# Attention values on half the TensorE columns, with unsplit F32 rows and a ring of probability tiles

## What is computed

```python
q_big = rope(einsum('bshk,hkq->bshq', (hidden_q @ Wq.T), w_kc_q))       # 192 per head
kv_r = rope(kv_c)                                                       # 1444 x 64
scores = einsum('bhsr,bhlr->bhsl', q_big @ W_qr, kv_r @ W_kr)
attn = softmax(scores)
ctx_c = einsum('bhsl,bld->bhsd', attn, kv_r)
out = reshape(einsum('bhsd,hkd->bhsk', ctx_c, w_kc_kv)) @ Wo.T
```

## Time and profile before

| | us |
|---|---|
| median of 3 runs | 2302.54 |
| the profiled execution, its own time | 2283.25 |
| its span | 2281.4 |
| PE busy | 1857.9 (81%) |
| PEld busy | 1632.6 (72%) |
| DVE busy | 1492.1 (65%) |
| ACT busy | 1220.5 (53%) |
| POOL busy | 1117.1 (49%) |

### The profile page before, as it was taken

The page is one execution under the profiler, slowest core; times in us unless marked ns, Lnnn a source line. Parts: engine busy times, 40 slices in busy tenths (PEclk is TensorE's granted clock), DMA queues, the critical chain, the costliest instruction groups (busy, mean ns, idle before and its releaser), DMA issues. The chain is left out here.

```text
span 2281.4 us, 38538 instructions
## 1 busy us (share of the span) xinstructions
PE 1857.9 (81%) x10550; PEld 1632.6 (72%) x10550; DVE 1492.1 (65%) x2799; ACT 1220.5 (53%) x2996; POOL 1117.1 (49%) x961
## 2 busy tenths in 40 slices
PE   4999958999999999999999973499993689837870
PEld 3677736888888888888888963499993466626870
DVE  4677777777777777767776433377774466656763
ACT  2111115777777767767777851366661266515650
POOL 0455528888788888878888852300004100014005
PEclk9999967999999999999999985699996599958985
DMA  5522251111111111111110002455542100026654
GB/s 159 197 58 57 55 176 55 63 63 63 45 54 63 64 31 63 63 64 63 63 54 11 16 8 78 140 197 196 204 165 58 34 1 0 0 77 196 198 164 113
DMA packets 115748, 195.76 MB, mean 86 GB/s; under 512 B 48213, under 2 KB 94265, under 8 KB 110161
## 3 DMA queue, kind: packets, MB, share of 16 engines
q1 hardware_dynamic: 107409, 180.88, 24.6%
q0 software_dynamic: 8192, 13.15, 2.0%
HBM read 147.01 MB, written 46.63 MB: 85 GB/s over the span
## 5 line engine op out<-in xcount | busy, mean ns | idle before, releaser
L501 POOL TENSOR_TENSOR EL<-E,EH 128x400 fp32r<-128x400 f32 x688 | 833.4, 1239 | 158.5 <-ACT EH L733 154.0
L599 DVE TENSOR_REDUCE PM<-bank 128x1 f32<-128x482 f32 (+1 forms) x624 | 397.2, 650 | 185.9 <-PE bank L578 182.9
L742 ACT ACTIVATE E<-bank 128x400 f32<-128x400 f32 x768 | 386.4, 503 | 212.8 <-PE bank L793 153.2
L733 ACT ACTIVATE EH<-E 128x400 fp32r<-128x400 f32 x768 | 407.0, 532 | 0.0
L175 PE MATMUL bank<-EH,KVH 128*128 128x400 f32 x768 | 283.1, 369 | 19.8 <-POOL EL L501 18.5
L578 PE MATMUL bank<-KH,QS 128*128 128x482 f32 (+1 forms) x624 | 250.9, 414 | 53.9 <-DVE KVL L549 27.6
L1248 POOL DMA_INDIRECT m_back<-rows_out,m_slots x64 | 64.8, 1013 | 450.8 <-DMA rows_out<-m_ys 421.2
L792 PE MATMUL bank<-QS,KH 128*128 128x400 f32 x768 | 272.1, 354 | 14.9 <-issue 9.1
L793 PE MATMUL bank<-QB,KB 66*128 66x400 f32 x768 | 269.1, 350 | 0.0
L175 PE MATMUL bank<-EH,KVL 128*128 128x400 f32 x768 | 265.7, 346 | 0.0
L175 PE MATMUL bank<-EL,KVH 128*128 128x400 f32 x768 | 265.5, 346 | 0.0
(11 more groups left out here) (244 smaller groups left out, 3983.3 us busy)
## 6 DMA issues: line engine op xcount, KB each, us to landing
m_stage_u<-in_m_up SPq DMA_DIRECT2D x20, 1392.0 KB
raw<-in_ctx_T SPq DMA_DIRECT2D x16, 1444.0 KB, 6.1
m_xg<-rows_in SPq DMA_DIRECT2D x55, 256.0 KB, 4.1
rows_out<-m_ys SPq DMA_DIRECT2D x55, 256.0 KB, 3.7
m_stage_d<-in_m_down SPq DMA_DIRECT2D x20, 696.0 KB
queries<-q_out SPq DMA_DIRECT2D x64, 200.0 KB, 2.4
QS<-queries SPq DMA_DIRECT2D x16, 800.0 KB, 6.1
rows_in<-zeros SPq DMA_DIRECT2D x5, 1792.0 KB
```

Of the source, the lines that this page charges most:

```text
L501: ops.tensor_tensor(EL[:, n % PB, :], E[:, n % EB, :], as_f32(EH[:, n % PB, :]), ALU.subtract).then_inc(sem, 1)
L599: nc.vector.tensor_reduce(PM[:, f:f + 1], psum[F0 + f % f_banks(b)][:, 0:KW[f % KC]], AX.X, ALU.max).then_inc(red_done, 1)
L733: nc.scalar.activation(EH[:, n % PB, :], E[:, n % EB, :], ACT.Copy).then_inc(hi_done, 1)
L742: nc.scalar.activation(E[:, n % EB, :], psum[S0 + n % SB][:, 0:CH], ACT.Exp).then_inc(exp_done, 1)
```

## The change

1. PSUM is one tensor `banks`, so that one instruction can read two banks.
2. Queries: `M2` keeps 64 columns a head. `narrow` takes two heads at a time, head `2j` to PSUM rows 0 to 63 and head `2j+1` to rows 64 to 127. ScalarE and VectorE then take a pair in one instruction of 128 rows, and four DMAs of 64 rows send it.
3. Attention: a step is a tile of 128 keys by 800 columns, even heads in one bank and odd heads in the next (24 steps). One exponential of 128x800 writes both into the ring `R`, where the four tiles of a group and a running sum lie innermost, so neighbouring columns stand 20 bytes apart. No `EH`, `EL`.
4. `values`: two F32 matmuls of 400 columns with 64 stationary columns, even heads to PSUM rows 0 to 63, odd heads to rows 64 to 127 of one bank `CTX`, from `KV` in F32.
5. Row sums: VectorE sums the even heads, four parts of 100 columns for each group of four tiles (`sum_even`); GpSimd adds the odd heads tile by tile (`sum_odd`); TensorE adds over the partitions with a matrix of ones (`sums`).
6. Maxima: two pieces of 482 columns in two banks, one `tensor_reduce` over both (`reduce_pair`, 20 instead of 39). With two banks in all, a pair waits for the reduction of the pair before.
7. Ten rotation parts go to GpSimd, two stay on VectorE. `KB` and `QB` have 128 rows, with a row that masks the padded keys, and the setup clears them.

The core of the diff:

```diff
@@ latent_queries
-                def narrow(c, h):
-                    pe.wait_ge(rot_done, c * H + (BUFS + h + 1))
-                    pe.wait_ge(lo_done, c * H + (h + 1))
+                def narrow(c, j):
+                    pe.wait_ge(rot_done, c * H + (BUFS + 2 * j + 2))
+                    pe.wait_ge(lo_done, c * HP + (j + 1))
                     for half in range(2):
-                        last = nc.tensor.matmul(psum[4 + h % 2][:, 0:CH], M2[:, half, h, :], rot[:, h % TURNS, half, :],
-                                                start=half == 0, stop=half == 1)
+                        for o in range(2):
+                            h = 2 * j + o
+                            last = nc.tensor.matmul(psum[4 + j % 2][o * DC:(o + 1) * DC, 0:CH], M2[:, half, h, :],
+                                                    rot[:, h % TURNS, half, :], start=half == 0, stop=half == 1)
                     last.then_inc(qq_ready, 1)
...
@@ latent_attention
+        def tiles_of(n):
+
+            return R[:, n // GT % 2, :, :, 1 + n % GT]
...
+            nc.vector.tensor_reduce(PM[:, 2 * i:2 * i + n], banks[:, k:k + n, 0:KW], AX.X, ALU.max).then_inc(red_done, 1)
...
+        def sum_even(v, b, g, part):
+
+            cols = slice(part * PC, (part + 1) * PC)
+            p, q = divmod(g, KT // GT)
+            if part == 0:
+                v.wait_ge(exp_done, b_val(b) * NS + ((g + 1) * GT + SB))
+            v.wait_ge(even_sum, b_val(b) * NG * PARTS + (PARTS * (g + 1) + part + 1))
+            src = R[:, g % 2, 0, cols, (1 if q == 0 else 0):]
...
+            nc.vector.tensor_reduce(out, src, AX.X, ALU.add).then_inc(even_sum, 1)
...
+            nc.gpsimd.tensor_tensor(out, first, tile_of(n, 1), ALU.add).then_inc(odd_sum, 1)
...
+            for o in range(2):
+                last = nc.tensor.matmul(psum[MISC][o * DC:(o + 1) * DC, 0:CH], ones[:], ES[:, p, o, :], start=True, stop=True)
+            last.then_inc(sum_done, 1)
...
+        def context_out(act, b, p):
+            act.wait_ge(av_done, b_val(b) * NS + (EB + KT * (p + 1)))
+            act.wait_ge(ct_ready, b_val(b) + 1)
+            nc.scalar.activation(CU[:, p, :], psum[CTX][:, 0:CH], ACT.Copy).then_inc(cu_done, 1)
...
-                    split_products(nc, psum[A0 + g % 2][:, 0:CH],
-                                   [(KVH[b_mod(b)][:, cols], KVL[b_mod(b)][:, cols], EH[:, n % PB, :], EL[:, n % PB, :])],
-                                   first=t == 0, last=t == KT - 1).then_inc(av_done, 1)
+                    for o in range(2):
+                        last = nc.tensor.matmul(psum[CTX][o * DC:(o + 1) * DC, 0:CH], KV[b_mod(b)][:, t, :], tile_of(n, o),
+                                                start=t == 0, stop=t == KT - 1)
+                    last.then_inc(av_done, 1)
...
+                v.wait_ge(rows_set, BUFS)
                 for r in range(BUFS):
+                    v.memset(as_f32(QB[r][0:1, :]), 1.0)
+                    v.memset(as_f32(KB[r][0:3, :]), 1.0).then_inc(rows_set, 1)
+                v.wait_ge(rows_set, 2 * BUFS)
+                for r in range(BUFS):
+                    v.memset(as_f32(KB[r][0:1, 0:SK]), 0.0)
+                    v.memset(as_f32(KB[r][0:1, SK:]), PAD).then_inc(pads, 1)
```

More of the change, by code:

```diff
@@ L52, in __init__ @@
         self.nc, self.ctx = nc, ctx
-        self.psum = [ctx.enter_context(nc.psum_tensor(f"bank{i}", [P, PSUM_COLS], F32)) for i in range(8)]
+        self.banks = ctx.enter_context(nc.psum_tensor("banks", [P, 8, PSUM_COLS], F32))
+        self.psum = [self.banks[:, i, :] for i in range(8)]
         self.stats = fixed(ctx, nc, "stats", [S, B, 6])
@@ L425, in latent_attention @@
-        KVL = [fixed(ctx, nc, f"KVL{r}", [P, KT * KS + P - KS], F32R) for r in range(BUFS)]
+        KB = [fixed(ctx, nc, f"KB{r}", [P, SKP], F32R) for r in range(BUFS)]
+        KV = [fixed(ctx, nc, f"KV{r}", [P, KT, DC]) for r in range(BUFS)]
         raw = fixed(ctx, nc, "raw", [P, 2, SK])
@@ L578, in max_piece @@
-            nc.tensor.matmul(psum[F0 + f % banks][:, 0:KW[j]], QS[r][:, t * P:(t + 1) * P],
-                             KH[r][:, sum(KW[:j]):sum(KW[:j + 1])], start=True, stop=True).then_inc(f_ready, 1)
+                pe.wait_ge(red_done, b_val(b) * NP)
+            for f in pieces(i):
+                t, j = divmod(f, KC)
+                last = nc.tensor.matmul(psum[f_bank(b, i) + f % 2][:, 0:KW], QS[r][:, t * P:(t + 1) * P],
+                                        KH[r][:, KAT[j]:KAT[j] + KW], start=True, stop=True)
@@ L581, in turn_max @@
+            last.then_inc(f_ready, 1)
         def turn_max(pe, b):
@@ new lines, in sum_odd @@
+        def sum_odd(pool, b, n):
+            p, t = divmod(n, KT)
+            if t == 0:
+                return
+            pool.wait_ge(exp_done, b_val(b) * NS + (n + 1 + SB))
+            done = b_val(b) * 2 * ADDS + (p * ADDS + t - 1)
+            if t > 1 or p or b is not FIRST:
+                pool.wait_ge(odd_sum, done)
+            if t == KT - 1 and b is not FIRST:
+                pool.wait_ge(sum_done, b_val(b) * 2 + (p - 1))
+            first = tile_of(n - 1, 1) if t == 1 else EA[:]
+            out = ES[:, p, 1, :] if t == KT - 1 else EA[:]
+            nc.gpsimd.tensor_tensor(out, first, tile_of(n, 1), ALU.add).then_inc(odd_sum, 1)
@@ new lines, in sums, with sums_out @@
+        def sums(pe, b, p):
+            pe.wait_ge(even_sum, b_val(b) * NG * PARTS + (2 * PARTS + PARTS * (NG // 2) * (p + 1)))
+            pe.wait_ge(odd_sum, b_val(b) * 2 * ADDS + ADDS * (p + 1))
+            if p == 0 and b is not FIRST:
+                pe.wait_ge(su_done, b_val(b) * 2)
+            for o in range(2):
+                last = nc.tensor.matmul(psum[MISC][o * DC:(o + 1) * DC, 0:CH], ones[:], ES[:, p, o, :], start=True, stop=True)
+            last.then_inc(sum_done, 1)
+        def sums_out(act, b, p):
+            act.wait_ge(sum_done, b_val(b) * 2 + (p + 1))
+            if b is not FIRST:
+                act.wait_ge(sr_in, b_val(b) * 32)
+            nc.scalar.activation(SU[:, p, :], psum[MISC][0:DC + 1, 0:CH], ACT.Copy).then_inc(su_done, 1)
@@ L668, in steps @@
             body(Batch(0, B - 1), False, False)
+        LAST = Batch(0, B - 1)
         with nc.Block() as block:
@@ L756, in step @@
-                    high(b, NS - 1)
+                            act.wait_ge(odd_sum, odd_sums_to(before(b), NS + n - EB))
+                        k = S0 + 2 * (n % SB)
+                        nc.scalar.activation(tiles_of(n), banks[:, k:k + 2, 0:CH], ACT.Exp).then_inc(exp_done, 1)
+                        if n in HI_AT and has_keys:
+                            keys_high(act, b + 2, HI_AT.index(n))
+                        if n == 2 * SUM_AT + 1 and b is not FIRST:
+                            sums_out(act, before(b), 1)
@@ L784, in step @@
[L784 to L794 removed]
+                        pe.wait_ge(cu_done, b_val(b) * 2 + (p + 1))
@@ L805, in step @@
-                        if n == TURN_AT and has_next:
+                        if has_next and 2 * m < NP:
+                            max_pair(pe, b + 1, 2 * m)
+                        if m == 0:
+                            if b is not FIRST:
+                                for n in range(NS - 2, NS):
+                                    values(before(b), n)
+                            pe.wait_ge(m_in, b_val(b) * 32 + 32)
+                        for n in (2 * m, 2 * m + 1):
+                            scores(b, n)
@@ L808, in step @@
                             turn_max(pe, b + 1)
-                steps(pe, step)
-                for n in range(NS - BEHIND, NS):
-                    values(Batch(0, B - 1), n)
-                project(pe, Batch(0, B - 1))
+                        for n in (2 * m - 2, 2 * m - 1):
+                            if n >= 0:
+                                values(b, n)
+                        if m == SUM_AT and b is not FIRST:
+                            sums(pe, before(b), 1)
+                        if m == SUM0_AT:
+                            sums(pe, b, 0)
+                        if m == OUT_AT and b is not FIRST:
+                            pe.wait_ge(su_done, b_val(b) * 2 + 1)
+                            project(pe, before(b))
+                steps(pe, step)
+                for n in range(NS - 2, NS):
+                    values(LAST, n)
+                pe.wait_ge(res_done, B - 1)
+                sums(pe, LAST, 1)
+                pe.wait_ge(su_done, 2 * B)
+                project(pe, LAST)
             @block.vector
```

406 lines of the change are left out of this document (196 added, 210 removed).

## The result

The changed kernel takes 2447.56 us, the median of 4 runs (2435.74 to 2454.26), beside 2301.54 us for the kernel before (2293.95 to 2312.28, 4 runs): a ratio of 1.0625, 95% interval 1.0561 to 1.069. It is 146 us slower where I had forecast 93 us faster. The profiled execution took 2453.29 us of its own time, with a span of 2451.5 us.

What follows compares the result with a forecast made beforehand. TensorE was taken as the bound, GpSimd 6 us a batch behind; fifteen batches -69, last batch -10, queries -21, folding -3, start +10 gave -93 us, from 2302.5 to 2209 us, with an 8-in-10 range of 2065 to 2455.

Steps and rivals of the forecast that it cites:

- the price of a slot: TensorE's F32 matmuls: one record of 400 columns was put at 0.335 us, called a slot.
- `divide`: Attention, once a batch: the context copy waits for VectorE's divide, costing TensorE 2 us (between 0 and 2.3).
- rival 2: Attention values: moving rows read at a 20-byte step come at half speed, 0.67 us a record; 2531 us, chance 0.09.
- The overlap: F32 matmuls on two column halves: eight records of two steps take 5 slots, between bounds of 4 and 8.
- rival 3: TensorE: the column halves overlap fully, 4 slots, and switching is free; 2051 us, chance 0.15.
- rival 1: TensorE: the column halves don't overlap, 8 slots a block; 2445 us, chance 0.19.
- Switching: TensorE changing between 128 and 64 stationary columns: 0.16 us a switch, two switches or 0.32 us per two steps.
- Maxima: Attention: a pair's banks are free after 1.81 us, the next is issued after 1.91; TensorE's waits put at nothing.
- GpSimd: Attention: 22 additions of 1.26 us and ten rotation parts, 43 us a batch, hidden; idle a quarter of the time.
- Last batch: Attention's final batch, which has no maxima: 49 us for 59, so -10 us.
- Queries and folding: Stages before the attention: 32 pairs of heads save 21 us, and the folding saves 3 us.
- Start: Start of the attention: new setup memsets delay the rotations by 10 us (bounds 5 to 15).

Runs made afterwards that it cites:

- The ruler: Changed kernel with TensorE and GpSimd inputs at steps of 1 to 8 elements, ScalarE output 1 to 5, beside the ring, attention not computed: 2312.37 us.
- the square: Changed kernel and its unit-step-ring version, each with halves apart (2447.56, 2157.55 us) and with both value matmuls on one half (2958.7, 2400.51 us).

## Why the prediction was wrong

**The step that failed is the price of a slot.** I took "0.335 us a record of 400 columns" from the earlier trace rows, records that read `rotated` at unit step, and put it on records that read `R` with 20 bytes from column to column. The right price is 0.71 us from start to start, 0.72 with what switching adds to the block (2.88 / 4). With it and with the four slots that the halves really take, my own sheet gives 57.9 + 12 x (2.88 - 1.68) = 72.3 us a batch; the trace has 72.15. The last tenths of that are chance: the sheet still has 0.7 us too much for `sums` (three slots, where they take two) and 0.6 for `divide`, and 1.2 us of waits for the maxima too little.

**I had that mechanism as rival 2 and gave it 0.09**, on the argument that an F32 record spends twice an F32R one's time, "so that half the reading speed is spare". No row said that. The ruler shows that it isn't so: 516 ns at unit step go to 884 at a step of 16 bytes. Rival 2's 2531 us was too high mainly because I kept five slots in it. The prediction had also doubled ScalarE's time for the same step, as a doubt, and never TensorE's outside this rival.

**The overlap** was to be 5 slots of 8 and is 4 (rival 3). It was the question on which I said that all hangs; the square shows it to be worth 14.9 us a batch at unit step. The question was right, and the answer erred to the safe side.

**The time fell inside the range by luck.** The forecast was faster, with 0.70 on that sign and 2255 us as the end of its own case; the kernel is 6% slower. 2447.56 lies below 2455, the upper end, only because that end was there for rival 1, halves that don't overlap, at 2445 us. Rival 1 is false. Only the profile tells the two apart: eight records of 0.36 us one after another would also make 2.9 us a block, but the records are of 0.9 us, in pairs.

The other terms, point by point:

- *Switching*: 0.32 us per two steps. In the query timeline above the F32R matmuls beside the block stand 0.09 and 0.08 us further apart than 0.184, and the block takes 0.15 over its four slots: 0.32. In the attention the maxima pair ahead of the values takes 0.60 for 0.44 and the pair behind them 0.54 for 0.44, so it is 0.4 rather than 0.32 there. Nearly right.
- *`divide`*: 2 us a batch. TensorE waits 19.1 us in 14 batches for the copy, 1.4 us; the copy itself 60.8 us for `divide`, 4.3 each. Right in kind; 1.4 for 2 us.
- *Maxima*: "just fits". TensorE's matmuls wait 17.6 us for them from 370 to 1430 us, 1.2 us a batch. The margin of 0.1 us wasn't there, a sign of being wrong that the prediction had named. It cost little here, and up to 3 us a batch (42.1 us of TensorE's matmuls in the run with three contexts, of 370 to 1180 us) once the values are fast.
- *ScalarE*: 0.83 us an exponential, "Were the 20-byte step of the output to double it, 40: hidden still". It doubled, ACT is busy 601 of 1082 us, 40 us a batch, and it is hidden: right.
- *GpSimd*: 1.26 us an addition, measured 1.25, from two errors that cancel. It is 1.04 at unit step without VectorE's two-input instructions, and the step adds 0.21. POOL's idle time is 43%, for a forecast of a quarter, because the batch got longer.
- *Last batch*: -10. Last `turn_max` to the last projection is +9.8 with the step and, at unit step, 69.0 us for 79.9: -10.9. Right but for the slot, although it was summed with five slots for four.
- *Queries and folding*: -24. Measured -22.3 in the trace, -24 by itself. Five slots were again four: the blocks of a pair of heads stand 6.03 us apart for 7.05 before, where I had 6.4. Part of what that gives is lost between the groups, where two such distances together take 15.7 us for 15.1; there the granted clock also falls to 0.50 for 3.4 us (122.6 to 126.0 for one), which it didn't before (1.00 from 80 to 303 us). From the first pair's block to the last pair's it is 24.5 us less.
- *Start*: +10. First memset to first rotation was 12.7 us and is 27.3: +14.6. Timeline of VectorE after, start of the attention:

```profile
298.36 1.45 DVE L894 MEMSET QB<- 1x1664 f32 x1 [0.40 <-DVE KB L891]
300.07 1.34 DVE L895 MEMSET KB<- 3x1536 f32 x1 [0.27 <-issue]
...
312.98 3.29 DVE L529 TENSOR_TENSOR raw<-raw,ropeT 128x722 f32<-128x722 f32 x4
```

Memsets of one row cost the 0.87 ns a column that I took. What I counted too small are the gaps between them, 0.25 to 0.4 us fifteen times, 4.9 us. To the first `turn_max` the growth is 15.7 us, just over the 15 that bounded this term.

At unit step the result is 0.946 of the kernel before, against a forecast of 0.959 (2209 / 2302.5). The sheet with four slots a block and two for each of the `sums` has 57.9 - 12 x 0.335 - 0.7 = 53.2 us a batch, and the run 55.5: waits for the maxima, put at nothing, and the dearer switching are most of the difference.

## What to carry to other kernels

When a layout is chosen so that one engine can sum its neighbours, price every other reader and writer of it at that step: here VectorE saved 0.3 us on each of 24 sums a batch, and TensorE paid 0.37 us on each of 48 slots. A price taken from a trace holds for the access pattern it was measured with; if the pattern differs, the difference is a term of the sum of its own, or the bounds must hold the doubled price. And two rivals can give the same time, so look at the profile for the mechanism before you call a number confirmed.

## What the runs showed of the hardware

- F32 matmuls on the two column halves overlap fully: eight records of 400 columns in 1.49 us to the next start, against 2.83 us on one half. With rows at a step of 20 bytes it is 2.98 against 5.83.
- A TensorE record of 400 F32 columns lasts 516, 527, 704, 884, 895, 878 and 904 ns at steps of 1, 2, 3, 4, 5, 6 and 8 elements. At unit step it already costs 0.335 us from start to start, where an F32R matmul of 400 columns costs 0.184; at 20 bytes it costs 0.71.
- ScalarE's output has the same staircase: 839, 896, 1249 and 1616 ns for 800 columns at steps of 1 to 4. GpSimd's input has a lower one: 1040, 1146, 1246 ns at steps of 1, 3 and 4.
- VectorE's reduction to 100 columns takes 563 ns over four neighbours and 665 over five, and 843 and 1022 to 1031 ns when they lie 1600 bytes apart.
- A VectorE addition of two tiles of 400 columns takes 556 ns at best and 1111 at the median in a kernel in which GpSimd adds and rotates; GpSimd's additions grow from 1040 to 1242 ns.
